# A recurrent decoder layer on Trainium2: a new order of the side work in a group of sixteen steps

## The chip, the cores and the metric

The kernel runs on one core of a Trainium2 chip. The metric is the device time in microseconds of one execution; the median of several executions counts. The engines are TensorE (PE; its weight loads are PEld), VectorE (DVE), ScalarE (ACT), GpSimd (POOL) and SyncE (SP), which issues most of the DMAs.

## What is computed

A decoder layer over x of 16 batches x 128 time steps x 256 features. Its first part is a recurrence over the 128 time steps, beside it attention and a mixture of experts:

```python
def step(carry, inp):
    h_ssm = silu(h_ssm @ A.T + bxt)                  # state of 64
    y_ssm = h_ssm @ Cw.T + Cb + dxt
    r = sigmoid(i_r + h_r); z = sigmoid(i_z + h_z)   # h_* = h_rnn @ W_hh.T, GRU state of 128
    n = tanh(i_n + r * h_n)
    h_rnn = (1 - z) * n + z * h_rnn
    fused = g0 * y_ssm + g1 * (h_rnn @ proj_w.T)     # g = sigmoid(x @ gate_w.T)
```

Then x1 = layernorm(x + fused); a retention layer (queries of x1, keys and values of ctx_1024, a rotary embedding, a decay mask) gives x2 = layernorm(x1 + ret); eight experts with the top 2 of 8 and a capacity of 320 rows work on x2; the sum is normalised once more.

## The kernel before, in words

The work is ordered by hand. A group g has CH = 16 time steps: two tiles j = 0, 1 of ST = 8 steps x 16 batches = 128 rows. There are 8 groups. Each engine runs its own list: in a group, for every step s, first the step of the recurrence (`rec`), then the side work that the list has for s. Groups 0 and 1 stand alone, because keys and values are computed in them; groups 2 to 7 are a loop (A and M true). Engines meet only by semaphores, which count up.

One step of the recurrence: TensorE multiplies the state (`at_w`) and the two halves h1, h2 of the GRU state (float16, high and low) by the weights (rec, L783 to L812); ScalarE takes two sigmoids (L549, L550) and the tanh (L552); VectorE does a scan (L1131), two small ops (L1133, L1134), the state product (L1137), the scans that give h1 and hist (L1142, L1143), and h2 (L1145). TensorE's part of step s needs VectorE's h2 of step s - 1. So side work stands in front of the next step on the same engine.

Side work of group g in the loop, by the step behind which it stands:

- TensorE (`iteration`, L917): `fin_a` and `fin_b` of tile 2g - 1 at 0 and 1 and of tile 2g at 12 and 13 (output of both states, and at the end of `fin_b` the gate matmuls into the bank TB); `scores` of chunk g - 2 at 2, 4; inputs of the next tiles at 3, 5, 14, 15; `x1_tr` at 6; `mix` at 7, 9; `q_proj` at 8, 10, both halves into TB; `back` at 11. `fin_b` at 13 waits for the rotation (qmul_ready).
- VectorE (L1280): stats and norm of x1 at 0, 1 and 4, 5; `fuse` at 2, 3 and 14, 15; `decay` at 5; two `residual` at 10; two pairs of rotation products at 11, 12; statistics and variance of x2 at 13; `logits` and `norm_2` at 14, 15, one tile each.
- ScalarE (L612): `gates` at 1, 13; `ret_high` at 6; x1T copies at 7; x1R copy at 11; `q_high` at 14.
- GpSimd (L431), in one queue and as soon as its inputs are there: `rstd_1` twice, `ret_low`, `rot_q` (two sums of 128x256), `rstd_2`, `q_low` (two differences).

Names used below: TB, FB, QB, SC are PSUM banks; `pv_ready`, `res_ready`, `x1_ready` and the like are the semaphores that a named result raises. The kernel splits float32 operands in float16 high and low halves: `q_high`, `q_low`, `ret_high`, `ret_low`. The order around it:

```python
            with act.Fori(2, CHUNKS) as g:
                iteration(g, True, True)
            gates(TILES - 1)
            ret_high(CHUNKS - 2)
            x1T_copy(CHUNKS - 1)
```

Of the kernel before, what the change touches and what calls it, by code (L numbers as in the profile page):

```python
# [14 lines left out]
SSM, RNN = 64, 128  # L15
# [26 lines left out]
V_SLOTS = (2, 4, 6, 7, 9, 11)  # L42
# [4 lines left out]
LO_STEP = (2, 3, 4, 5, 6, 6, 7, 7, 8, 8, 9, 9, 10, 13, 13, 14)  # L47
# [14 lines left out]
def mk_decoder_kernel(nc, xtok, xT, ctxT, consts, AbE, BwT, CwE, DwT, W_ihT, b_rows, bsel, iota, W_hhT, projT,  # L62
# [5 lines left out]
    with ExitStack() as ctx:  # L68
# [93 lines left out]
        rs1 = sb("rs1", [P, 1])  # L162
        x1 = [sb(f"x1_{j}", [P, D]) for j in range(2)]
# [68 lines left out]
        def quarter(a1, a2, p):  # L232
# [164 lines left out]
        def _(pool):  # L397
# [16 lines left out]
            def rot_q(c):  # L414
                for h, op in enumerate((ALU.subtract, ALU.add)):
                    pool.wait_ge(q["qmul_ready"], 2 * c + h + 1)
                    pool.tensor_tensor(qr[:, h, :], tm[:, 2 * h, :], tm[:, 2 * h + 1, :], op).then_inc(q["qr_ready"], 1)  # L417

            def q_low(c):
                for h in range(HD):  # L420
                    pool.wait_ge(q["qh_ready"], 2 * c + h + 1)
                    pool.tensor_tensor(qp[1][:, h, :], qr[:, h, :], qp[0][:, h, :], ALU.subtract).then_inc(q["ql_ready"], 1)
# [8 lines left out]
            def iteration(g, A, M):  # L431

                if A:
                    rstd_1(2 * g - 2)
                    if not M:
                        rot_k(3)
                    rstd_1(2 * g - 1)
                if A and not M:

                    for i in range(8):  # L440
                        pool.dma_start(ybuf[i * 4 * P:(i + 1) * 4 * P, :].rearrange("(k p) d -> p k d", p=P),
                                       zero[:].unsqueeze(1).to_broadcast([P, 4, D])).then_inc(q["zrow"], 16)
                if M:
                    ret_low(g - 2)
                if A:
                    rot_q(g - 1)
                if M:
                    rstd_2(g - 2)
                if A:
                    q_low(g - 1)  # L450
# [8 lines left out]
            iteration(0, False, False)  # L459
# [3 lines left out]
            iteration(1, True, False)  # L463
            with pool.Fori(2, CHUNKS) as g:
                iteration(g, True, True)
            rstd_1(TILES - 2)
            rstd_1(TILES - 1)
            ret_low(CHUNKS - 2)
            rot_q(CHUNKS - 1)
# [75 lines left out]
        def _(act):  # L545
# [8 lines left out]
            def gates(n):  # L554

                act.wait_ge(q["fin_ready"], n + 1)
                for i in range(2):
                    nc.scalar.activation(gxs[:, i:i + 1], TB[:, i:i + 1], ACT.Sigmoid, bias=gb[:, i:i + 1]).then_inc(q["gx_ready"], 1)

            def x1T_copy(c):  # L560
                act.wait_ge(q["x1tr_ready"], c + 1)
                for h in range(HD):
                    nc.scalar.copy(x1T[:, h, :], TB[:, h * 256:(h + 1) * 256]).then_inc(q["x1T_ready"], 1)
# [1141 lines left out]
```

## Time and profile before

| | |
|---|---|
| median of 3 executions | 502.61 us (502.03 to 504.88) |
| profiled execution, its own time | 504.28 us |
| its span, first to last instruction | 502.4 us |
| mean granted TensorE clock | 0.896 of full speed |
| busy: PE, PEld, DVE, ACT, POOL | 404.9, 309.5, 382.6, 235.6, 138.5 us |
| first sigmoid of the recurrence, last one | 11.1 us, 279.3 us |

The three parts of the span are the recurrence with its side work (to 281 us), attention's rest and the routing (to about 330 us), and the experts and the final norm. A row of a timeline says when an instruction began, how long it took, and in brackets how long its engine had been idle before and what released it. Rows of one kind that follow each other are merged (x2, x48).

### The profile page before, as it was taken

How to read it: one execution, taken by the hardware profiler on the slowest of the kernel's cores; microseconds unless marked ns; L12 is line 12 of the kernel's file. 1: busy time of each engine (PE TensorE's matmuls, PEld its weight loads, DVE VectorE, ACT ScalarE, POOL GpSimd, SP SyncE). 2: the span in 40 equal slices, each digit the busy share in tenths (PEclk: the TensorE clock that was granted, in tenths of full speed). 3: DMA queues.
4: the chain of work that ended last, by engine and by line, in shares of the span. 5: the costliest groups of instructions: out<-in, count | busy, mean ns of one | idle time of the engine just before them, and what ended most of it. 6: DMA issues, size and time to landing. Idle time of an engine off the chain costs nothing.

```text
span 502.4 us, 13430 instructions
## 1 busy us (share of the span) xinstructions
PE 404.9 (81%) x4675; PEld 309.5 (62%) x4675; DVE 382.6 (76%) x1575; ACT 235.6 (47%) x803; POOL 138.5 (28%) x207
## 2 busy tenths in 40 slices
PE   7978899899999999999899766128999999998000
PEld 4535676687877878778687655115677777776000
DVE  5578888988879788797987555875789888894184
ACT  1454166433333332333333133334998888972053
POOL 0023332211113121121211221153124554413284
PEclk8889989999999999999999586557999999999555
DMA  8940128110111102011020000016534565101482
GB/s 289 359 172 1 33 74 294 31 37 1 52 32 31 52 0 80 3 31 52 0 76 1 23 3 22 22 35 213 168 137 149 182 214 198 47 7 48 145 281 104
DMA packets 38238, 46.49 MB, mean 93 GB/s; under 512 B 4283, under 2 KB 32702, under 8 KB 38202
## 3 DMA queue, kind: packets, MB, share of 16 engines
q1 hardware_dynamic: 34474, 35.93, 21.5%
q0 software_dynamic: 3200, 9.40, 5.9%
q10 hardware_dynamic: 528, 0.69, 0.5%
q8 instruction: 21, 0.34, 0.3%
q14 instruction: 15, 0.12, 0.1%
HBM read 35.04 MB, written 11.01 MB: 92 GB/s over the span
## 4 chain that ended last, share of the span: by engine, by line
PE 43%; DVE 27%; ACT 11%; issue 10%; POOL 3%; DMA 3%; ACTq 0%; SPq 0%; DVEq 0%; POOLq 0%
PE bank L758 42%; DVE h L1142 3%; DVE ub L1131 3%; DVE mb L1133 3%; ACT arena L676 2%; ACT arena L667 2%; DVE h L1145 2%; DVE hist L1143 2%; DVE st L1205 1%; ACT arena L705 1%; ACT kp L676 1%; DVE vp L1480 1%; DVE tm L1174 1%; DVE mb L1134 1%; PE bank L1056 1%
## 5 line engine op out<-in xcount | busy, mean ns | idle before, releaser
L549 ACT ACTIVATE rzb<-bank 128x32 f32<-128x32 f32 x128 | 25.4, 198 | 104.0 <-PE bank L758 102.7
L758 PE MATMUL bank<-h,whp 128*128 128x32 f16 x1143 | 62.0, 184 | 5.1 <-DVE h L1142 2.6
L758 PE MATMUL bank<-arena 128*128 128x320 f16 x384 | 57.0, 307 | 1.4 <-DVE arena L1527 1.4
L1131 DVE TENSOR_TENSOR_SCAN ub<-rzb,bank 128x32 f32<-128x32 f32 x128 | 28.0, 219 | 39.5 <-ACT rzb L549 38.4
L758 PE MATMUL bank<-arena,kp 128*128 128x320 f16 x384 | 54.5, 299 | 0.0
L758 PEld LDWEIGHTS bank<-h,whp 128*128 128x128 f16 x1143 | 41.7, 96 | 15.4 <-DVE h L1145 3.5
L552 ACT ACTIVATE nb<-ub 128x16 f32<-128x16 f32 x128 | 27.9, 218 | 47.4 <-DVE ub L1131 47.4
L758 PEld LDWEIGHTS bank<-arena 128*128 128x128 f16 x384 | 38.2, 101 | 16.9 <-DVE arena L1527 1.6
L758 PEld LDWEIGHTS bank<-hsb,at_w 66*64 66x64 f32 x256 | 25.2, 137 | 34.7 <-DVE hsb L1137 23.2
L758 PEld LDWEIGHTS bank<-arena,kp 128*128 128x128 f16 x384 | 37.3, 98 | 14.1
L758 PE MATMUL bank<-hsb,at_w 66*64 66x16 f32 x256 | 36.9, 220 | 6.9 <-DVE hsb L1137 6.7
L1133 DVE TENSOR_SCALAR mb<-rzb,hneg,hup 128x16 f32<-128x16 f32 x128 | 41.1, 321 | 0.0
L503 POOL DMA_INDIRECT ybuf<-arena,six x24 | 24.2, 1009 | 58.0 <-DVE arena L1542 53.1
L705 ACT ACTIVATE arena<-bank,b1s 128x320 f32<-128x320 f32 x64 | 32.2, 540 | 16.5 <-PE bank L758 16.4
L1531 DVE CAST arena<-arena 128x320 f16<-128x320 f32 x64 | 20.9, 326 | 19.8 <-ACT arena L705 18.1
L417 POOL TENSOR_TENSOR qr<-tm 128x256 f32<-128x256 f32 x16 | 11.6, 725 | 84.8 <-DVE tm L1174 84.8
L407 POOL TENSOR_TENSOR ve<-mv,epst 128x1 f32<-128x1 f32 (+1 forms) x24 | 5.0, 208 | 103.4 <-DVE mv L1162 78.9
L667 ACT ACTIVATE arena<-wbuf 128x1024 bf16<-128x1024 f32 x32 | 33.4, 1058 | 0.0
L1142 DVE TENSOR_TENSOR_SCAN h<-nb,mb 128x32 f16<-128x32 f32 x128 | 31.6, 247 | 1.5
L1535 DVE TENSOR_TENSOR arena<-arena 128x320 f16<-128x320 f32 x64 | 30.4, 485 | 0.0
L758 PE MATMUL bank<-xin_t,wih 128*128 128x128 f32 x192 | 28.6, 286 | 1.4 <-DMA bw<-in_BwT 1.4
L1145 DVE TENSOR_TENSOR h<-hist,h 128x16 f16<-128x16 f32 x128 | 25.4, 198 | 4.5
(209 smaller groups left out, 935.5 us busy)
## 6 DMA issues: line engine op xcount, KB each, us to landing
wbuf<-in_w SPq DMA_DIRECT2D x16, 1024.0 KB, 5.9
ybuf<-zero POOLq DMA_DIRECT2D x8, 512.0 KB, 7.2
wbuf<-ybuf SPq DMA_DIRECT2D x16, 256.0 KB, 5.5
xin_t<-in_xT SPq DMA_DIRECT2D x16, 128.0 KB, 2.2
arena<-in_ctxT SPq DMA_DIRECT2D x4, 512.0 KB, 7.0
xfin_t<-in_xT SPq DMA_DIRECT2D x16, 128.0 KB, 2.2
xres<-in_xtok SPq DMA_DIRECT2D x16, 128.0 KB, 2.1
x_d<-x SPq DMA_DIRECT2D x8, 256.0 KB, 2.3
```

The lines of the kernel that those rows point to most:

```text
L503: pool.indirect_dma_start(ybuf[:, :], bass.IndirectOffsetOnAxis(ap=six[0:m, col], axis=0), yt[e % 2][0:m, c, :], None, bounds_check=2 * S ...
L549: nc.scalar.activation(od(rzb[:]), RZ[j][:, s * 2 * B:(s + 1) * 2 * B], ACT.Sigmoid).then_inc(q["r_ready"], 1)
L552: nc.scalar.activation(od(nb[:]), od(ub[:]), ACT.Tanh).then_inc(q["n_ready"], 1)
L667: nc.scalar.activation(wjunk[p % 2].rearrange("p (a b) -> p a b", a=src.shape[1]), src, ACT.Square, accum_out=wsum2[j][:, p // 2, p % 2:p ...
L705: nc.scalar.activation(h32[:, f % 4, :], bank[2 + f % 4][:, 0:CAP], ACT.Relu, bias=b1s[j][:, f:f + 1]).then_inc(q["h32_ready"], 1)
L758: return nc.tensor.matmul(out_, lhsT, rhs, start=start, stop=stop, skip_group_check=True)
L1131: nc.vector.tensor_tensor_scan(ub[:], rzb[:, 0:2 * B], NS[j][:, s * 32:s * 32 + 32], 0.0, ALU.mult, ALU.add).then_inc(q["npre_ready"], 1)
L1133: nc.vector.tensor_scalar(ev(mb[:]), od(rzb[:, 2 * B:4 * B]), hneg[:, 0:1], hup[:, 0:1], ALU.mult, ALU.add)
L1142: nc.vector.tensor_tensor_scan(h1[:], nb[:], mb[:], 0.0, ALU.mult, ALU.add).then_inc(q["h1_done"], 1)
L1145: nc.vector.tensor_tensor(h2[:], h_of(j, s), od(h1[:]), ALU.subtract).then_inc(q["h2_done"], 1)
L1531: nc.vector.tensor_copy(hp[0][:, f, :], h32[:, f % 4, :]).then_inc(q["h_hi"], 1)
L1535: nc.vector.tensor_tensor(hp[1][:, f, :], h32[:, f % 4, :], hp[0][:, f, :], ALU.subtract).then_inc(q["h_lo"], 1)
```

## The change

It replaces the list of the loop by a new one on four engines, and changes a few helpers. In steps of the new loop:

- TensorE: `fin_a` 0 and 11, `fin_b` 1 and 13, `scores` 2, 3, inputs 4, 6, 14, 15, `x1_tr` 5, `mix` 7, 10, `q_proj` 8, 9, `back` 12.
- Gate matmuls move from the end of `fin_b` to `fin_a`, into columns 384, 385 of RZ[j]; the bias matmul goes the other way. `in_a` waits for the gates.
- `q_proj` writes its second half to FB; each half raises q_ready. `fin_a` of tile 2g waits for all rotation products.
- VectorE: products one by one at 8, 9, 9, 10; `residual` 10, 11; stats of x2 12, variance 13; `fuse` 1, 2 and 13, 14; stats of x1 0, 3; `norm_1` of the second tile 4; `ret_low` 6 (it was GpSimd's); both `logits` 15.
- ScalarE: `norm_1` of the first tile at 2, `norm_2` of both tiles at 15, as Identity with scale and bias; x1T copies at 6 and 7; x1R copy 12; `q_high` 13, 14. GpSimd computes the biases (`shift_1`, `shift_2`).
- GpSimd: `rot_q` and `q_low` wait for h2 of steps 11, 12, 13, 14 (`behind`). The two `rot_q` wait for all products.
- In group 1 the value matmuls of step 9 go to 10, three low halves go to step 11, the tables to 8, projections and products to 8, 9 and 9, 10.

```diff
-V_SLOTS = (2, 4, 6, 7, 9, 11)
+V_SLOTS = (2, 4, 6, 7, 10, 11)
-LO_STEP = (2, 3, 4, 5, 6, 6, 7, 7, 8, 8, 9, 9, 10, 13, 13, 14)
+LO_STEP = (2, 3, 4, 5, 6, 6, 7, 7, 8, 8, 11, 11, 11, 13, 13, 14)
...
-            def ret_low(c):
-                pool.wait_ge(q["rh_ready"], c + 1)
-                pool.tensor_tensor(rp[1][:], ret[:], rp[0][:], ALU.subtract).then_inc(q["rl_ready"], 1)
+            def rot_q(c, h):
+                pool.wait_ge(q["qmul_ready"], 2 * c + 2)
+                op = (ALU.subtract, ALU.add)[h]
+                pool.tensor_tensor(qr[:, h, :], tm[:, 2 * h, :], tm[:, 2 * h + 1, :], op).then_inc(q["qr_ready"], 1)
...
+            def shift_2(c):
+                pool.tensor_tensor(ng2[:], zero[:, 0:2], mv2[:, :, 0], ALU.subtract).then_inc(q["neg2"], 1)
+                pool.wait_ge(q["neg2"], c + 1)
+                pool.wait_ge(q["rstd2"], c + 1)
+                pool.tensor_tensor(nm2[:], ng2[:], rs2[:], ALU.mult).then_inc(q["shift2"], 1)
+            def behind(g, s):
+                pool.wait_ge(q["h2_done"], CH * g + s + 2)
+            def iteration(g):
+                rstd_1(2 * g - 2)
+                shift_1(g)
+                rstd_1(2 * g - 1)
+                behind(g, 11)
+                rot_q(g - 1, 0)
+                behind(g, 12)
+                rot_q(g - 1, 1)
+                behind(g, 13)
+                q_low(g - 1, 0)
+                rstd_2(g - 2)
+                shift_2(g - 2)
+                behind(g, 14)
+                q_low(g - 1, 1)
...
+            def norm_1(g):
+                act.wait_ge(q["shift1"], g - 1)
+                nc.scalar.activation(x1[0][:], s1b[:], ACT.Identity, bias=nm1[:], scale=rs1[:]).then_inc(q["x1_ready"], 1)
+            def norm_2(c, j):
+                if j == 0:
+                    act.wait_ge(q["shift2"], c + 1)
+                    act.wait_ge(q["lg_ready"], 2 * c + 2)
+                nc.scalar.activation(x2[:, bass.ds(2 * c + j, 1), :].rearrange("p o (h d) -> p (o h) d", h=HD), halves((QB, SC)[j]), ACT.Identity,
+                                     bias=nm2[:, j:j + 1], scale=rs2[:, j:j + 1]).then_inc(q["x2_ready"], 1)
...
             def in_a(n, j):
+                if not isinstance(n, int) or n >= 2:
+                    pe.wait_ge(q["gx_ready"], 2 * n - 2)
...
                 mm(FB[:, 0:D], xfin_t[j][:, 0, :], dw[:, 0, :], False, False)
+                for h in range(HD):
+                    last = mm(RZ[j][:, 3 * P:3 * P + 2], xfin_t[j][:, h, :], gw[:, h, :], h == 0, h == 1)
+                last.then_inc(q["gate_ready"], 1)
+            def fin_b(n, j):
+                mm(FB[:, 0:D], xfin_t[j][:, 1, :], dw[:, 1, :], False, True)
                 mm(FB[:, D:2 * D], ones16[:], bzq[:, RNN:RNN + D], False, False)
...
-                last.then_inc(q["fin_ready"], 1)
+                mm(FB[:, D:2 * D], od(hist[j][:]), pw[:], False, True).then_inc(q["fin_ready"], 1)
...
-                    last = mm(TB[:, o * 256:(o + 1) * 256], wq[:, h, o * P:(o + 1) * P], x1T[:, h, :], h == 0, h == 1)
-                if o == 1:
-                    last.then_inc(q["q_ready"], 1)
+                    last = mm((TB, FB)[o][:, 0:256], wq[:, h, o * P:(o + 1) * P], x1T[:, h, :], h == 0, h == 1)
+                last.then_inc(q["q_ready"], 1)
...
                 if part == 0:
                     dve.wait_ge(q["gx_ready"], 2 * n + 2)
+                    dve.wait_ge(q["fin_ready"], n + 1)
...
                     dve.wait_ge(q["fuse_a"], n + 1)
+                    if not isinstance(n, int):
+                        dve.wait_ge(q["x1_ready"], n)
...
             stats_1(n)
             norm_1(n, 1)
+            ret_low(c - 1)
```

## Rows read from the trace of the kernel before

**Rows 1.** the profile's page, part 4: the chain that ended last, by engine
```profile
PE 43%; DVE 27%; ACT 11%; issue 10%; POOL 3%; DMA 3%; ACTq 0%; SPq 0%; DVEq 0%; POOLq 0%
```

**Rows 2.** timeline, group 3, L549: start us, us taken, what [idle before <-releaser]
```profile
128.51 0.20 ACT L549 ACTIVATE rzb<-bank 128x32 f32<-128x32 f32 x1 [0.96 <-PE bank L758]
...
132.41 0.20 ACT L549 ACTIVATE rzb<-bank 128x32 f32<-128x32 f32 x1
...
139.41 0.20 ACT L549 ACTIVATE rzb<-bank 128x32 f32<-128x32 f32 x1 [0.96 <-PE bank L758]
...
141.56 0.20 ACT L549 ACTIVATE rzb<-bank 128x32 f32<-128x32 f32 x1 [1.09 <-PE bank L758]
...
148.55 0.20 ACT L549 ACTIVATE rzb<-bank 128x32 f32<-128x32 f32 x1 [0.96 <-PE bank L758]
...
150.84 0.20 ACT L549 ACTIVATE rzb<-bank 128x32 f32<-128x32 f32 x1 [0.89 <-PE bank L758]
...
152.57 0.20 ACT L549 ACTIVATE rzb<-bank 128x32 f32<-128x32 f32 x1 [0.96 <-PE bank L758]
...
155.02 0.20 ACT L549 ACTIVATE rzb<-bank 128x32 f32<-128x32 f32 x1
...
159.11 0.20 ACT L549 ACTIVATE rzb<-bank 128x32 f32<-128x32 f32 x1 [0.96 <-PE bank L758]
```

**Rows 3.** timeline, step 12 of the group, VectorE's h2
```profile
152.09 0.17 DVE L1145 TENSOR_TENSOR h<-hist,h 128x16 f16<-128x16 f32 x1
```

**Rows 4.** timeline, step 6: GpSimd's ret_low and VectorE's h2
```profile
140.55 0.67 POOL L426 TENSOR_TENSOR rp<-ret,rp 128x256 f16<-128x256 f32 x1 [1.68 <-ACT rp L578]
140.66 0.59 DVE L1145 TENSOR_TENSOR h<-hist,h 128x16 f16<-128x16 f32 x1
```

**Rows 5.** timeline of TensorE, step 11: back and the next state matmul
```profile
149.08 1.19 PE L758 MATMUL bank<-rgi,sT 128*128 128x136 f32 x8 [0.53 <-DVE sT L1198]
150.21 0.29 PE L758 MATMUL bank<-hsb,at_w 66*64 66x16 f32 x2
```

**Rows 6.** timeline, steps 12 and 13: L1133 and GpSimd's rot_q
```profile
151.28 0.33 DVE L1133 TENSOR_SCALAR mb<-rzb,hneg,hup 128x16 f32<-128x16 f32 x1
...
153.01 0.72 POOL L417 TENSOR_TENSOR qr<-tm 128x256 f32<-128x256 f32 x1 [1.44 <-DVE tm L1174]
153.01 0.76 DVE L1133 TENSOR_SCALAR mb<-rzb,hneg,hup 128x16 f32<-128x16 f32 x1
```

**Rows 7.** timeline, step 13: gate matmuls, next state matmul, the gates
```profile
153.95 0.50 PE L758 MATMUL bank<-gw,xfin_t 128*128 128x2 f32 x4
...
154.38 0.29 PE L758 MATMUL bank<-hsb,at_w 66*64 66x16 f32 x2
...
154.49 0.41 ACT L558 ACTIVATE gxs<-bank,gb 128x1 f32<-128x1 f32 x2 [1.15 <-PE bank L758]
```

**Rows 8.** timeline of VectorE, steps 13 and 15: statistics and a norm of x2
```profile
154.34 0.88 DVE L1205 BATCH_NORM_STATS2 st<-bank 128x6 f32<-128x128 f32 x4
...
159.26 0.54 DVE L1224 TENSOR_SCALAR x<-bank,mv,rs 128x256 f32 x1
```

**Rows 9.** line L1185 (VectorE's ret_low, after the loop): ns min/median/max
```profile
L1185 DVE TENSOR_TENSOR rp<-ret,rp x1: 426/426/426, 304.5 to 304.5; 128x256 f16<-128x256 f32 x1
```

**Rows 10.** timeline of TensorE, step 7: mix and the next state matmul
```profile
141.40 1.36 PE L758 MATMUL bank<-rp,vp 128*128 128x32 f16 x48
142.69 0.29 PE L758 MATMUL bank<-hsb,at_w 66*64 66x16 f32 x2
```

**Rows 11.** timeline of ScalarE near the end: two norms of the output
```profile
483.19 1.09 ACT L750 ACTIVATE arena<-arena,nm,rs 128x256 f32<-128x256 f32 x2 [1.12 <-POOL nm L535]
```

**Rows 12.** line L1278, group 1: low halves of the values (keys: 743 median, x8)
```profile
L1278 DVE SCALAR_TENSOR_TENSOR vp<-arena,scl,vp x8: 741/746/826, 78.5 to 95.6; 128x512 f16<-128x512 f32 x8
```

**Rows 13.** timeline of VectorE behind the loop: norm of x1
```profile
290.84 0.75 DVE L1167 TENSOR_SCALAR x<-s1b,mv,rs 128x256 f32<-128x256 f32 x1 [0.93 <-POOL rs L409]
```

**Rows 14.** groups by line and form, ScalarE: xcount | busy us, mean ns
```profile
L651 ACT ACT_TABLE_LOAD x1 | 1.3, 1283 | 2.3 <-issue 2.3
```

More of the change, by code:

```diff
@@ L428, in rstd_2, with shift_1 @@
             def rstd_2(c):
                 rstd(q["var2"], q["eps2"], rs2[:], None, q["rstd2"], (ve2[:], mv2[:, :, 1]), c + 1)
[L431 to L450, printed above, removed]
+            def shift_1(g):
+                pool.tensor_tensor(ng1[:], zero[:, 0:1], mv1[:, 0:1], ALU.subtract).then_inc(q["neg1"], 1)
+                pool.wait_ge(q["neg1"], g - 1)
+                pool.wait_ge(q["rstd1"], 2 * g - 1)
+                pool.tensor_tensor(nm1[:], ng1[:], rs1[:], ALU.mult).then_inc(q["shift1"], 1)
@@ L452, in _, with second @@
+            def second():
+                rstd_1(0)
+                rot_k(3)
+                rstd_1(1)
+                for i in range(8):
+                    pool.dma_start(ybuf[i * 4 * P:(i + 1) * 4 * P, :].rearrange("(k p) d -> p k d", p=P),
+                                   zero[:].unsqueeze(1).to_broadcast([P, 4, D])).then_inc(q["zrow"], 16)
+                for h in range(HD):
+                    rot_q(0, h)
+                for h in range(HD):
+                    q_low(0, h)
             pool.memset(ones[:], 1.0).then_inc(q["init_p"], 1)
@@ L458, in _ @@
                 rot_k(i)
-            iteration(0, False, False)
             pool.wait_ge(q["nrm_done"], 1)
             pool.tensor_tensor(inv[:], nrm[:], mhalf[:], ALU.pow).then_inc(q["inv_done"], 1)
-            iteration(1, True, False)
+            second()
             with pool.Fori(2, CHUNKS) as g:
-                iteration(g, True, True)
+                iteration(g)
             rstd_1(TILES - 2)
             rstd_1(TILES - 1)
-            ret_low(CHUNKS - 2)
-            rot_q(CHUNKS - 1)
+            for h in range(HD):
+                rot_q(CHUNKS - 1, h)
             rstd_2(CHUNKS - 2)
@@ L683, in _ @@
             exponentials(0, 0, TILES - 4)
-            q_high(CHUNKS - 1)
+            q_high(CHUNKS - 1, 0)
+            q_high(CHUNKS - 1, 1)
             x1R_copy(CHUNKS - 1)
@@ L915, in sums, with iteration, early @@
                 last.then_inc(q["nsum"], 1)
-            def iteration(g, A, M, has_next):
+            def iteration(g, has_next):
+                for s in range(CH):
+                    rec(g, s // ST, s % ST)
+                    if s == 0:
+                        fin_a(2 * g - 1, 1)
+                    if s == 1:
+                        fin_b(2 * g - 1, 1)
+                    if s in (2, 3):
+                        scores(g - 2, s - 2)
+                    if s == 4:
+                        in_a(2 * g + 1, 1)
+                    if s == 5:
+                        x1_tr(g - 1)
+                    if s == 6:
+                        in_b(1)
+                    if s in (7, 10):
+                        mix(g - 2, (s - 7) // 3)
+                    if s in (8, 9):
+                        q_proj(g - 1, s - 8)
+                    if s == 11:
+                        pe.wait_ge(q["qmul_ready"], 2 * g)
+                        fin_a(2 * g, 0)
+                    if s == 12:
+                        back(g - 2)
+                    if s == 13:
+                        fin_b(2 * g, 0)
+                    if has_next and s == 14:
+                        in_a(2 * g + 2, 0)
+                    if has_next and s == 15:
+                        in_b(0)
+            def early(g, A):
                 for s in range(CH):
```

224 lines of the change are left out of this document (126 added, 98 removed).

## The prediction

> **What bounds the kernel now.** I read the page first. Its chain of work gives TensorE 43% and VectorE 27%, with neither engine full [rows 1]. This is a chain of waits: 128 dependent steps of a recurrence. So I took the start of ScalarE's first sigmoid (L549) as the clock of a step and read group g = 3 of the loop (six looped groups, 2 to 7, repeat it within 0.1 us). The group takes 159.11 - 128.51 = 30.60 us for 16 steps [rows 2]. The step from 150.84 to 152.57 takes 1.73 us, and 141.56 to 148.55 is four steps at 1.75 [rows 2]. So 1.73 us is the floor: sigmoid at 0, VectorE's first scan at 0.30, h2 starting at 1.25 [rows 3], h2's matmuls, next sigmoid. Sixteen floors are 27.7 us. The group loses 2.9 us in named places, and 6 groups hold 17 us: this is all the change can win in the loop.
>
> The losses, as interval after a step minus 1.73:
> - Step 6, 2.15 (+0.42): GpSimd's ret_low starts at 140.55 for 0.67 us, and h2, due at 140.66, takes 0.59 instead of 0.17 [rows 4].
> - Step 11, 2.29 (+0.56): TensorE waits 0.53 us for the residual before `back` [rows 5]; the next step's state matmul is behind it.
> - Step 13, 2.45 (+0.72): GpSimd's rot_q begins together with L1133, which takes 0.76 us instead of 0.27; then `fin_b`, which waited for the rotation, still has the gate matmuls in it when the state is ready [rows 6, 7].
> - Steps 14 and 15, together 4.09 (+0.63) [rows 2], then step 0 (2.03, +0.30) and step 1 (1.87, +0.14), together 3.90 [rows 2]: VectorE does statistics (0.88 us) and in each of two steps fuse, logits and a 0.54 us norm [rows 8]. Room for VectorE's extras in a step is about 0.7 us, from h2's end to the next scan; above it the step grows one for one.
>
> **The change, part by part, per looped group.**
> *Step 6/7.* ret_low goes from GpSimd to VectorE: h2 is free, -0.42. But `mix` in step 7 needs it at once. VectorE starts it 0.09 after h2's start, at 1.33, it takes 0.43 [rows 9], and a matmul follows 0.06 behind: `mix` starts at 1.82, 0.09 after the next sigmoid. Today it starts 0.16 before the sigmoid, and at 1.29 us from its start to the state matmul's it just fits [rows 10]. So step 7 grows by 0.24. Net -0.18.
> *Steps 8 to 10.* Query halves go to two banks, so a rotation product starts behind each half; one, two, one products (0.33 us pitch) plus a residual stay within about 0.05 of the room. TensorE's two projections (1.1 us) fit. Net 0; cover: VectorE's 0.7 us. Without it, each extra 0.1 us is paid.
> *Steps 11, 12.* `fin_a` takes the gate matmuls (0.43 us pitch [rows 7]) and gives up the bias one (0.21): about 1.37 us on TensorE, 0.08 more than `mix`, so step 11 costs 1.84. `back` goes behind step 12, where the last residual is ready about as the sigmoid starts; its 1.13 us [rows 5] end 0.02 late. Step 12 costs 1.78 against 1.73. Net -0.41.
> *Step 13.* The rotation is over three steps earlier, `fin_b` loses the gates, gates come from `fin_a` of step 11 (0.41 us [rows 7] on ScalarE behind q_high's 0.4; room there is 1.1). Four statistics in step 12 make the scan of 13 late by 0.06. GpSimd's rot_q now waits for h2: start 1.25 + 0.17 + 0.08 = 1.50, 0.72 long, over at 0.49 of the next step. In step 12 of today one runs from the sigmoid at 150.84 on and is over at 0.72; L1133 took 0.33, and the step was still 1.73 [rows 2, 6]. So it costs nothing with 0.2 in hand. Step 13: 1.80, net -0.65. VectorE's fuse is split over 13 and 14, and 14 drops to 1.75, -0.20.
> *Step 15.* Here is the new cost. The norms of x2 go to ScalarE, after step 15's tanh and before the next group's first sigmoid, and they wait for both logits (same PSUM banks). VectorE issues logits behind h2 with dynamic addresses: about 1.44 and 1.62, 0.22 long like today's, over at 1.84. ScalarE then sees the semaphore (0.06), computes an address (0.1) and runs two Identity activations of 128x256. Today two such take 1.09 us [rows 11], the next op about 0.09 earlier; from PSUM they may be 0.1 to 0.2 cheaper (the 128x256 copies out of PSUM are 0.37). I take 0.95: next sigmoid at 2.95, and 0.05 for q_low(1), which GpSimd can only start behind the rstd_2 and shift_2 chain, so near 0.03 of step 15, over at 0.70. Step 15: 3.0 instead of 2.14, **+0.86**. Bounds: 2.2 if the wait costs VectorE's old excess only, 3.3 if nothing overlaps.
> *Steps 0, 1.* VectorE no longer has a norm in step 15: step 0 is 1.74 (-0.29); TensorE is ahead of the late sigmoid, so `fin_a` is covered. Step 1 has a shorter `fin_b`: 1.77 (-0.10). x1's norm on ScalarE in step 2 (0.59) is ready as VectorE wants s1b at 1.33; the shift chain on GpSimd is over some 0.6 us before it. Rests of 0.01 to 0.03 in steps 2 to 5 and 9: +0.07.
> Sum without step 15: -0.18 - 0.41 - 0.65 - 0.20 - 0.29 - 0.10 + 0.07 = -1.76; six groups, -10.6. Step 15 counts in five (behind the last the norms cover matmuls): +4.3. **Loop: -6.3.**
> *Second group (g = 1).* Low halves of keys and values (0.74 us each, 16 of them [rows 12]) move from steps 9, 10 to 11, so three stand together there, and tables join two of them in step 8: 2.2 and 2.05 us against 0.7 of room. The value matmuls go to neighbouring steps 10 and 11, where they overlap VectorE's excess less. Followed step by step, +1.4 at step 11, +0.75 at the end after the faster step 13. Bounds 0 and +2.
> *After the loop.* `fin_a` of the last tile no longer waits for a fuse: -0.9; x1's norm, 0.75 today beside ret_low on GpSimd instead of 0.41 [rows 13], -0.34; GpSimd's first rotation sum waits for all four products: +0.62. **-0.6**, bounds -1.3 and +0.6. First group: its changes end in a wait for GpSimd's rot_k, 0. SP's and POOL's queues: loads of xfin wait for fuses that come earlier; the store of x2 waits for ScalarE's norms, needed only a group later.
> Sum: -6.3 + 0.75 - 0.6 = **-6.1 us**. The profiled execution took 504.28, of which 502.40 is span; it becomes 498.2. The median, 1.7 lower at 502.61, becomes **496.5**.
>
> One cost the rows leave open: var_2 (step 13) reads SBUF as q_low begins. Held like h2 it pushes fuse, +0.5 a group, to 499.5. The Trainium skill (GPSIMD Engine Reference, Specifications) names as contended only VectorE instructions in a 2-port mode or with two SBUF inputs; the row of L1133 (0.76) agrees; by that, this cost would be 0.
>
> **Rivals.**
> - *ScalarE's hold is cheap.* Step 15 near 2.2: 0.8 x 5 = 4 less, 492.5. For: activations run beside TensorE's lead. Against: the sigmoid stands behind both norms in one queue. 15%.
> - *It balances out.* Two collisions a group left (0.44 each, 5.3 in all), or the second group at +2 with var_2 held: 500.5 to 502. 17%.
> - *GpSimd still meets VectorE (slower).* Place: the four big subtractions of steps 11 to 15, started behind h2. If the wait and its arithmetic let each begin late enough to sit on L1133 or h2, each costs about 0.44 [rows 4, 6]: 1.76 x 6 = 10.6, less 0.3 that the sum has for it, 506.8. It decides from about 0.5 us of lateness; my slack is 0.2, and nil for q_low(1). For: q_low(1) waits for a long chain. Against: these waits are short today (0.08). 10%.
> - *Identity needs its own table (slower).* A table load takes 1.28 us [rows 14]; the trace has two in all, this one ahead of the sigmoids and one at the exponentials. Two swaps and back per group are 5.1 us, 31 in all, 527. Square and copies ran beside the sigmoid without one, Identity never did. 3%. The Trainium skill (ScalarE: Activation LUTs, Table sets) says that the cheap functions, identity among them, are in every set; by that this rival falls.
> - *It does not do what it says* is in the second one: the parts move costs, and only the sum moves time.
>
> **Numbers.** Forecast case 55%, 494 to 499.5. With cheap hold 15%: faster by over 0.5% (about what a measurement of this kernel can tell from no change; below 500.1) 0.70. Same 0.17, slower 0.13. The range 491 to 502.5 leaves out the two slower cases and a little at the bottom.
>
> **What would show it.** In the changed profile: step 6 at 1.73 with h2 at 0.17; a TensorE wait for ret_low and 2.0 in step 7; 1.84 in step 11, 1.8 in step 13; L1133 never above 0.35 in the loop; after step 15 some 3.0, ScalarE waiting for logits, two norms of 0.5; group length near 29.7; group 1 longer. Wrong: step 15 below 2.5, L1133 or h2 above 0.5 us, or a table load in the loop.

## The result, and the profile after

The changed kernel takes 512.82 us in the median of 4 executions (509.92 to 517.02). The kernel before takes 503.75 us in 4 executions beside it. The ratio is 1.018, with a 95% interval of 1.0133 to 1.0228: the change costs 1.8%, where 1.2% less time was forecast. The profiled execution took 509.92 us, with a span of 508.1 us; it is the fastest of the four. Here and below a median is of all executions, while a ratio leaves out those over 1.5% above the fastest of their kernel (two each of kernels 1 and 4, four of kernel 5), so that it can lie up to 0.4% beside the quotient of the medians.

The page's list of the chain that ended last, by engine, looks almost like the old one [rows 1]:

```profile
PE 44%; DVE 23%; ACT 13%; issue 12%; POOL 3%; DMA 3%; ACTq 1%; SPq 0%; DVEq 0%; POOLq 0%
```

VectorE lost 4 points, as the change meant it to; ScalarE and "issue" took 2 each, TensorE 1, and none of them stands out. So I measured steps again, from one first sigmoid (L571 now) to the next. The loop's groups, which were equal within 0.13 us before, no longer are:

| group | 0 | 1 | 2 | 3 | 4 | 5 | 6 | 7 (15 steps) |
|---|---|---|---|---|---|---|---|---|
| before, us | 45.19 | 41.47 | 30.7 | 30.6 | 30.6 | 30.6 | 30.6 | 28.44 |
| after, us | 43.29 | 43.48 | 33.58 | 31.26 | 30.26 | 33.83 | 31.25 | 27.08 |

The stretches of the loop show what differs. The columns are start and end, the busy time (with the number of instructions) of PE, PEld, DVE, ACT and POOL, the granted TensorE clock, the DMA share and GB/s. The kernel before, from group 2 on:

```profile
98.00:129.00 31.00, 29.18 (x455) 24.36 (x456) 25.86 (x139) 10.47 (x60) 5.81 (x11) 1.00 0.09 27
129.00:159.00 30.00, 28.59 (x454) 23.82 (x453) 25.26 (x138) 10.15 (x56) 5.76 (x11) 1.00 0.11 35
159.00:190.00 31.00, 29.11 (x458) 24.17 (x455) 26.26 (x142) 10.67 (x60) 5.77 (x11) 1.00 0.11 34
190.00:220.00 30.00, 28.59 (x451) 23.86 (x451) 25.27 (x138) 10.15 (x56) 5.77 (x11) 1.00 0.12 35
220.00:251.00 31.00, 29.23 (x459) 24.23 (x457) 26.26 (x141) 10.54 (x60) 5.77 (x11) 1.00 0.11 34
```

The same view of the changed kernel, one row for each of groups 2 to 6:

```profile
98.00:131.00 33.00, 32.26 (x460) 26.33 (x461) 24.75 (x138) 10.84 (x60) 5.84 (x14) 0.90 0.12 34
131.00:163.00 32.00, 30.74 (x460) 25.24 (x459) 24.41 (x137) 12.32 (x63) 5.80 (x14) 0.95 0.12 37
163.00:193.00 30.00, 28.93 (x453) 23.93 (x453) 24.43 (x137) 11.32 (x62) 5.80 (x14) 1.00 0.11 33
193.00:227.00 34.00, 32.94 (x457) 27.02 (x457) 24.71 (x137) 11.75 (x62) 5.85 (x14) 0.85 0.11 32
227.00:258.00 31.00, 29.95 (x456) 24.57 (x455) 24.41 (x137) 11.33 (x62) 5.80 (x14) 0.94 0.10 32
```

Before, the granted clock is 1.00 in every row. After, it is 1.00 only in group 4, which is also the only short one. The order of the clocks (1.00, 0.95 and 0.94, 0.90, 0.85) is the order of the lengths (30.26, 31.26 and 31.25, 33.58, 33.83).

**Where the clock falls.** The timeline of TensorE at the start of group 5, over the first two steps:

```profile
193.03 0.50 PE L815 MATMUL bank<-gw,xfin_t 128*128 128x2 f32 x4
194.18 0.29 PE L815 MATMUL bank<-hsb,at_w 66*64 66x16 f32 x2 [0.66 <-DVE hsb L1215]
194.42 0.61 PE L815 MATMUL bank<-h,whp 128*128 128x32 f16 x9
194.85 1.20 PE L815 MATMUL bank<-dw,xfin_t 128*128 128x256 f32 x2
...
196.05 1.06 PE L815 MATMUL bank<-pw,hist 128*128 128x256 f32 x2
```

and the windows around it, with the columns as above:

```profile
190.00:194.00 4.00, 3.53 (x37) 2.95 (x36) 2.33 (x15) 1.81 (x8) 1.03 (x4) 1.00 0.35 98
194.00:198.00 4.00, 3.82 (x39) 2.63 (x40) 2.74 (x15) 0.96 (x8) 1.08 (x4) 0.57 0.00 0
```

TensorE has run ahead: `fin_a` (192.08 to 193.53) began 1.2 us before the late sigmoid (193.27) and is over long before step 0 has given TensorE its next input, the state product `hsb` at 194.13. So it stands still for 0.66 us. In the kernel before this matmul follows `fin_a` without a stop. Behind that the two 128x256 matmuls of `fin_b` take 1.20 us; at 192.59, ahead of the stop, the same form takes 0.60. This is the lower of the two levels, 1.2 instead of 2.4 GHz. `fin_b` is on the path then, and step 1 takes 2.84 us instead of 1.76. The timeline of ScalarE shows why the sigmoid was late, and the long step 1 (195.02 to 197.86):

```profile
192.36 1.02 ACT L605 ACTIVATE x<-bank,nm,rs 128x256 f32 x2 [1.21 <-DVE lg L1306]
193.27 0.20 ACT L571 ACTIVATE rzb<-bank 128x32 f32<-128x32 f32 x1
...
195.02 0.20 ACT L571 ACTIVATE rzb<-bank 128x32 f32<-128x32 f32 x1 [0.98 <-PE bank L815]
...
197.86 0.20 ACT L571 ACTIVATE rzb<-bank 128x32 f32<-128x32 f32 x1 [1.76 <-PE bank L815]
```

The first row is the hold, which the prediction had priced at +0.86 for step 15: two Identity norms behind `logits`, 1.02 us long, with the sigmoid of step 0 behind them.

A second place is step 11. Group 4 (first three rows) has the clock at 1.00, group 5 (the others) loses it:

```profile
182.34 0.42 DVE L1255 TENSOR_TENSOR tm<-bank,cq 128x256 f32<-128x256 f32 x1
183.01 0.67 PE L815 MATMUL bank<-cwe,hsb 66*128 66x256 f32 x2 [0.26 <-DVE tm L1255]
183.52 0.60 PE L815 MATMUL bank<-dw,xfin_t 128*128 128x256 f32 x2
...
214.27 0.67 PE L815 MATMUL bank<-cwe,hsb 66*128 66x256 f32 x2 [0.26 <-DVE tm L1255]
214.77 0.97 PE L815 MATMUL bank<-dw,xfin_t 128*128 128x256 f32 x2
...
216.96 2.16 PE L815 MATMUL bank<-rgi,sT 128*128 128x136 f32 x8
```

`fin_a` waits for the last rotation product of step 10. The product ends at 182.76, as the h matmuls do, and `fin_a` starts 0.25 behind it: step 11 takes 2.26. In group 5 `back` takes 2.16 us instead of 1.17, and steps 11, 12 and 13 take 3.12, 2.73 and 2.59 instead of 2.26, 1.74 and 1.82.

**The 5.7 us of span, term by term.** Group 2 without the fall of the clock is 31.38 us (step 0 as 2.24, from the first experiment below), and groups 3 to 6 are 30.26 each, as group 4 is: 152.4 for five, against 153.0 before. The clock has added 160.18 - 152.4 = 7.8 us to them, and 4.01 - 2.74 = 1.3 to step 10 of group 1. The rest of group 1 is +0.7, group 7 is -1.4, and behind the last sigmoid it is 222.7 instead of 223.1, -0.4. Group 0 and what is ahead of it are 1.6 shorter, which is scatter: group 0 took 43.3 in one profile and 46.2 in another of one and the same kernel (the hold alone, below). Sum: -0.6 + 7.8 + 1.3 + 0.7 - 1.4 - 0.4 - 1.6 = +5.8.

This explains one execution, the fastest. The medians differ by 9.1 us, and the other three executions have a mean granted clock of 0.864 to 0.877 where the profiled one has 0.883. More clock lost in them would fit; there is no profile of them.

### The profile page after: what moved, and what is told of

It is laid out like the page before. It is cut to its first block, busy times and chain, and to the rows that moved or that the text cites. A ratio compares the mean times of both kernels' runs of the same rounds, so it can differ in the third digit from the quotient of the medians.

```text
span 508.1 us, 13545 instructions
## 1 busy us (share of the span) xinstructions
PE 414.0 (81%) x4675; PEld 315.0 (62%) x4675; DVE 373.3 (73%) x1564; ACT 242.8 (48%) x821; POOL 139.2 (27%) x224
## 4 chain that ended last, share of the span: by engine, by line
PE 44%; DVE 23%; ACT 13%; issue 12%; POOL 3%; DMA 3%; ACTq 1%; SPq 0%; DVEq 0%; POOLq 0%
PE bank L815 43%; DVE h L1220 2%; DVE ub L1209 2%; ACT arena L723 2%; DVE mb L1211 2%; ACT arena L732 2%; ACT kp L732 2%; ACT arena L762 2%; ACT rzb L571 1%; DVE hist L1221 1%; DVE tm L1255 1%; DVE vp L1587 1%; DMA wbuf<-ybuf 1%; DMA bw<-in_BwT 1%; DVE mb L1212 1%
## 5 line engine op out<-in xcount | busy, mean ns | idle before, releaser
L571 ACT ACTIVATE rzb<-bank 128x32 f32<-128x32 f32 x128 | 25.5, 199 | 111.3 <-PE bank L815 111.2
L815 PE MATMUL bank<-h,whp 128*128 128x32 f16 x1143 | 63.2, 185 | 4.2 <-DVE h L1220 2.6
L1211 DVE TENSOR_SCALAR mb<-rzb,hneg,hup 128x16 f32<-128x16 f32 x128 | 36.7, 286 | 0.0
L517 POOL DMA_INDIRECT arena<-x_d,gix x24 | 26.6, 1108 | 7.4 <-issue 6.3
```

Source lines behind the costliest of these rows:

```text
L517: pool.indirect_dma_start(xe[e % 2][0:m, c, :], None, x2_d[:, :], bass.IndirectOffsetOnAxis(ap=gix[0:m, col], axis=0), bounds_check=S - 1, ...
L571: nc.scalar.activation(od(rzb[:]), RZ[j][:, s * 2 * B:(s + 1) * 2 * B], ACT.Sigmoid).then_inc(q["r_ready"], 1)
L815: return nc.tensor.matmul(out_, lhsT, rhs, start=start, stop=stop, skip_group_check=True)
L1211: nc.vector.tensor_scalar(ev(mb[:]), od(rzb[:, 2 * B:4 * B]), hneg[:, 0:1], hup[:, 0:1], ALU.mult, ALU.add)
```

## The experiments

The theory is that the moves themselves gain a little, and that the loss is TensorE's clock, which falls behind the stops that the change makes: ScalarE's hold at the border of two groups, and `fin_a`'s wait at step 11. The rivals are that the hold and the wait cost by their own length, and that GpSimd still meets VectorE. No experiment changes what is computed; 2, 3 and 9 add matmuls or copies that nothing reads. "Before" is the kernel before, on the same chip; experiments 1 to 4 share one chip, 5 to 9 another. The change itself was not measured again on either, so its +1.8% stands beside these ratios and not in a row with them.

**1. The hold goes.** ScalarE writes the norms of x2 behind step 0 of the next group. For that, group 2 is taken out of ScalarE's loop, and the norms of the last looped group stand behind it. A part of the edit:

```diff
+                    if late and s == 0:
+                        norm_2(g - 3, 0)
+                        norm_2(g - 3, 1)
...
-                    if s == 15:
-                        norm_2(g - 2, 0)
-                        norm_2(g - 2, 1)
```

> The changed kernel, with ScalarE's two norms of x2 behind the first step of the next group instead of behind the last step of this one, so that no sigmoid stands behind the wait for the logits. Theory A (the hold of 1.1 us at the group's border leaves TensorE idle, and the granted clock then falls to 1.2 GHz for a stretch): the interval after step 15 goes from 2.9 to 1.8 us and the stretches at half clock in groups 2 to 7 are gone; the looped groups take 29.2 us each, the time falls by about 14 us, to 498. Theory B (the half-clock stretches have nothing to do with the hold): only 1.1 x 5 = 5.5 us are gained, 507, and half-clock stretches remain in the loop.

Measured: 505.25 us (10 executions) against 505.43, ratio 0.9989 [0.9935, 1.0043]. Step 15 is 1.74, step 1 is 1.73 or 1.74 in every looped group, and none loses the clock at its start. Step 0 grew to 1.98: `fin_a` with the gate matmuls is 1.37 us long, and no late sigmoid hides it now. Undisturbed groups are 29.32. Two groups still lose the clock, both at step 11 (3.14 and 3.17 instead of 2.26). So neither expectation came true: no fall is left at the borders, but falls are left in the loop, and the time is 505 instead of 498. The windows of this kernel, groups 4 and 5:

```profile
161.00:193.00 32.00, 31.59 (x461) 26.37 (x460) 24.73 (x138) 11.70 (x61) 5.89 (x14) 0.89 0.11 33
193.00:222.00 29.00, 28.59 (x453) 23.77 (x450) 24.13 (x136) 11.70 (x61) 5.83 (x14) 1.00 0.12 36
```

**2. The hold stays, the stop goes.** TensorE gets four unused 512-column matmuls where it would stand still.

```diff
                     if s == 0:
                         fin_a(2 * g - 1, 1)
+                        for i in range(4):
+                            mm(TB[:], ones16[:], no)
```

> The changed kernel with four matmuls of 512 columns into a free bank behind fin_a of step 0 (0.9 us of work that nobody reads, where TensorE is idle during ScalarE's hold). Theory A: the hold stays at 2.9 us, but the half-clock stretches at the starts of groups are gone; looped groups are 30.3 us each (up to 0.2 more for the extra matmuls), the time falls by 5 to 9 us, to 504 to 508. Theory B: half-clock stretches remain, the time is 512 to 514.

Measured: 503.41 us (10) against 505.43, ratio 0.9994 [0.9946, 1.0042]. The hold is as long as ever (step 15: 2.88 to 2.90, in group 2 3.09), and step 1 is 1.73 to 1.77 in every looped group. One group loses the clock, at step 11 (32.85), the others of groups 3 to 6 take 30.25. With more work on TensorE and a hold as long as ever the kernel stands level with the one before: the hold's length alone doesn't make these moves slower than the old order.

**3. The hold in the kernel before.** ScalarE waits for h2 behind step 15 and makes four unused copies.

```diff
+                    if M and s == 15:
+                        act.wait_ge(q["h2_done"], CH * g + CH + 1)
+                        for i in range(4):
+                            nc.scalar.copy(junk[:, i, :], zero[:])
```

> The kernel before with a hold of ScalarE alone: behind step 15 of each looped group it waits for h2 and makes four copies of 128x256 that nobody reads, 1.3 us. Theory A: the interval after step 15 grows by about 1.0 us to 3.1, and beside that half-clock stretches appear behind it in some groups, 1 us or more each: slower by 7 to 14 us against before. Theory B: 1.0 x 5 = 5 us slower, the granted clock stays at 1.00 in the loop.

Measured: 512.92 us (6) against 505.43, ratio 1.0146 [1.0065, 1.0226]. Step 15 is 3.09 to 3.22 instead of 2.14, and in three groups step 1 is 3.06 to 3.29 instead of 1.87, with the clock down. Those groups take 33.31, 33.56 and 33.56, an undisturbed one 31.24. The hold alone, with nothing else of the change, brings a loss. By this profile 3.2 us of it are the hold's own length (undisturbed groups are 0.65 longer, group 2 is 0.9 longer, group 7 0.3 shorter) and 6.7 us the three falls; it is the slowest of the six executions, so most of them lost less to the clock.

**4. GpSimd doesn't wait for h2.** `behind` does nothing.

```diff
             def behind(g, s):
-                pool.wait_ge(q["h2_done"], CH * g + s + 2)
+                pass
```

> The changed kernel without GpSimd's waits for h2 (its sums and differences begin as soon as their inputs are there). If these waits do what their name says, L1133's op or h2 is held in one to three places a group again, 0.3 to 0.5 us each: slower by 2 to 9 us than the changed kernel. If GpSimd was never the cost in the new order, the time stays within 1 us of the changed kernel's 512.

Measured: 509.54 us (10) against 505.43, ratio 1.0053 [1.0001, 1.0106]. Undisturbed groups are 30.70 instead of 30.26: step 12 is 1.86 instead of 1.74, step 13 is 2.15 instead of 1.82. The timeline of this kernel, GpSimd's rows each with the VectorE row beside it:

```profile
187.22 1.42 POOL L421 TENSOR_TENSOR qr<-tm 128x256 f32<-128x256 f32 x2 [11.51 <-DVE tm L1255]
187.58 0.40 DVE L1211 TENSOR_SCALAR mb<-rzb,hneg,hup 128x16 f32<-128x16 f32 x1
...
192.40 0.67 POOL L425 TENSOR_TENSOR qp<-qr,qp 128x256 f16<-128x256 f32 x1 [3.76 <-ACT qp L594]
192.51 0.59 DVE L1223 TENSOR_TENSOR h<-hist,h 128x16 f16<-128x16 f32 x1
```

With the waits, in the changed kernel, GpSimd starts behind h2 and is over in time, and L1211 keeps its 0.27:

```profile
186.27 0.18 DVE L1223 TENSOR_TENSOR h<-hist,h 128x16 f16<-128x16 f32 x1
186.53 0.73 POOL L421 TENSOR_TENSOR qr<-tm 128x256 f32<-128x256 f32 x1 [1.45 <-DVE h L1223]
...
187.28 0.27 DVE L1211 TENSOR_SCALAR mb<-rzb,hneg,hup 128x16 f32<-128x16 f32 x1
```

So the waits are worth 0.44 us a group. The rival that GpSimd still meets VectorE falls. The forecast of the time failed: 2 to 9 us more than the change were expected, and it is 3.3 less (509.54 against 512.82, on another chip, with ranges that overlap). The missing waits can't be the reason. The clock can: within the loop this profile lost it in group 2 alone, and the mean over the ten executions is 0.893. This kernel has kept both stops (0.64 to 0.85 us at the start of groups 3 to 7, 0.25 at step 11), so how often the clock falls behind them varies by more than a single repair gives back.

**5. The products come earlier.** Two pairs, at steps 8 and 9, so that `fin_a` at 11 waits for none of them.

```diff
-                    if s == 8:
-                        turn(g - 1, 0, 0)
-                    if s == 9:
-                        turn(g - 1, 0, 1)
-                        turn(g - 1, 1, 0)
+                    if s in (8, 9):
+                        rotate(g - 1, s - 8)
                     if s == 10:
-                        turn(g - 1, 1, 1)
                         residual(g - 2, 0)
```

> The changed kernel with the rotation products in pairs behind steps 8 and 9 instead of one, two, one behind 8, 9 and 10, so that fin_a of step 11 finds them done. Theory A (any stop of TensorE, also the 0.3 us in front of fin_a of step 11, can be followed by a stretch at 1.2 GHz): step 11 goes from 2.26 to 1.84 us, no half-clock stretch begins at a step 11 any more, those at the groups' starts remain; undisturbed groups 29.85 us; 3 to 6 us faster than the changed kernel. Rival: the stop at step 11 is only its own 0.42 x 6 = 2.5 us, and half-clock stretches still begin there.

Measured: 507.59 us (12) against 506.08, ratio 1.0003 [0.9957, 1.0049]. Step 11 is 1.94, step 9 is 1.84 (it was 1.73), the undisturbed group 30.01. No group loses the clock at step 11; groups 2, 3, 4 and 6 lose it at their start. So 1.94 is what `fin_a`'s length alone costs, and its wait cost 0.32.

**6. Both stops go** (1 and 5 together; no new edit).

> e1 and e5 together: ScalarE's norms behind step 0 of the next group, products at 8 and 9. Theory A: both stops are gone, no half-clock stretch in groups 2 to 7, each 28.9 us; about 10 us faster than before. Rival (the clock falls because the shorter list leaves TensorE less busy on the whole): half-clock stretches somewhere in groups 2 to 7, time 498 to 503.

Measured: 498.5 us (6) against 506.08, ratio 0.9831 [0.9781, 0.9881]: now 1.7% faster than before. Groups 3 to 6 take 29.10 each. Kernel 5, on the same chip, takes 9.1 us more; 4.9 of them are the hold's own length (0.91 in groups 3 to 6, 1.4 in group 2, less 0.1 in group 7), the rest goes with the mean clock, 0.889 there and 0.899 here. That the shorter list as a whole leaves TensorE too little to do falls with it: groups 3 to 7 keep the full clock. Windows, from group 1 on:

```profile
81.00:99.00 18.00, 15.08 (x122) 11.41 (x120) 14.89 (x63) 8.85 (x35) 2.71 (x4) 0.91 0.33 111
99.00:131.00 32.00, 31.32 (x453) 25.72 (x454) 24.53 (x137) 10.63 (x59) 5.83 (x14) 0.89 0.09 27
131.00:161.00 30.00, 29.77 (x468) 24.80 (x467) 25.29 (x143) 11.70 (x61) 5.78 (x14) 1.00 0.13 39
161.00:190.00 29.00, 28.77 (x455) 24.11 (x454) 24.32 (x138) 11.69 (x61) 5.82 (x14) 1.00 0.12 36
```

What is left of lower clock up to the last sigmoid lies ahead of step 0, in groups 0 and 1 and at the start of group 2, where neither edit reaches; kernels 1, 7 and 8 had none at the start of group 2 in their profiles, with the same code there. Against the kernel before, each on its own chip, the change stands at +1.8%, kernel 4 with the same two stops at +0.5%, the kernels with one stop gone at -0.1 and 0.0, with both gone at -1.7%.

**7. Two more repairs.** The norms of x2 one behind step 0 and one behind step 1; projections at 7 and 9, `mix` at 8 and 10, so that `ret_low` has a step of its own; both x1T copies at 6. A part of the edit:

```diff
-                    if s in (7, 10):
-                        mix(g - 2, (s - 7) // 3)
-                    if s in (8, 9):
-                        q_proj(g - 1, s - 8)
+                    if s in (8, 10):
+                        mix(g - 2, (s - 8) // 2)
+                    if s in (7, 9):
+                        q_proj(g - 1, (s - 7) // 2)
```

> e6 with the two norms split over steps 0 and 1, and with mix and projections exchanged (projections 7 and 9, mix 8 and 10, both x1T copies behind step 6), so that mix no longer waits for ret_low. Expected: step 0 from 1.98 to 1.75, step 7 from 2.02 to 1.75, groups of 28.4 us, 3 us faster than e6. If the waits only move (projection waits for the copies, scores for the norm), groups of 28.7 to 28.9 us.

Measured: 496.1 us (6) against 506.08, ratio 0.9804 [0.976, 0.9849]. Step 7 is 1.73 instead of 2.02, groups 4 to 6 are 28.81 to 28.83. The 2.4 us to kernel 6 are within what the two sets of six executions scatter. Step 0 stays 1.98, so it was not the length of the two norms but `fin_a`: its matmuls run from 183.95 on, and the state matmul stands behind them at 185.32.

**8. Group 1 as well.** Its three low halves spread over steps 9, 10 and 11, the tables at 9, the products at 10 and 11. A part of the edit:

```diff
-LO_STEP = (2, 3, 4, 5, 6, 6, 7, 7, 8, 8, 11, 11, 11, 13, 13, 14)
+LO_STEP = (2, 3, 4, 5, 6, 6, 7, 7, 8, 8, 9, 10, 11, 13, 13, 14)
```

> e8 with the low halves of group 1 spread over steps 9, 10, 11 one each, the tables at 9 and the products at 10 and 11. If the three low halves together at step 11 and the tables with two of them at step 8 cost what the prediction said (0.75 us) and the stop of TensorE there calls a half-clock stretch, group 1 goes from 42.8 to 41.5 us and the time falls by 1 to 2 us. Rival: the same work costs the same wherever it stands, 0.

Measured: 496.26 us (6) against 506.08, ratio 0.9792 [0.9747, 0.9838]. Step 9 of group 1 is 2.19 instead of 3.02, but steps 11 and 12 take back 0.3; the group is 42.17 instead of 42.68. From kernel 7 the time can't be told apart; 1 to 2 us less were expected, and 41.5 for the group.

**9. The hold with the stop filled, in the kernel before**, and the hold alone once more beside it. This is kernel 3 with the four unused matmuls of kernel 2.

```diff
                     if A and s == 0:
                         fin_a(2 * g - 1, 1)
+                        if M:
+                            for i in range(4):
+                                mm(TB[:], ones16[:], no)
```

> The kernel before with the same hold of ScalarE behind step 15, and now also with four unused 512-column matmuls on TensorE behind fin_a of step 0 of the looped groups, where TensorE stood still. Clock theory: the hold itself stays (step 15 at 3.1), but no stretch at half clock follows it, step 1 is 1.87 in every looped group, the looped groups are 31.25 to 31.65 long, and the time is 5 to 8 us below that of the kernel with the hold alone, about 508. If the lower clock came from the hold's length or from anything else than TensorE's standing still: two or three groups of 33.3 as before, and no gain over the kernel with the hold alone.

> The kernel before with the hold alone, once more, so that the filled one stands beside it on one chip. Both theories: step 15 at 3.1; a median near 513, 1.5% above the kernel before. Clock theory: step 1 at 3.1 with a stretch at half clock in two to four of the looped groups, not always the same ones.

Measured, against 504.6: filled 510.22 us (6), ratio 1.0125 [1.0085, 1.0166]; hold alone 513.1 (6), ratio 1.0181 [1.0145, 1.0218]. Windows of the hold alone, a group without and a group with a fall:

```profile
98.00:128.00 30.00, 28.22 (x451) 23.73 (x451) 24.68 (x132) 11.25 (x60) 5.82 (x11) 1.00 0.09 25
128.00:161.00 33.00, 30.95 (x453) 25.54 (x452) 25.75 (x139) 11.10 (x62) 5.79 (x11) 0.90 0.10 32
```

and of the filled one, the same two groups:

```profile
98.00:131.00 33.00, 31.23 (x475) 25.72 (x476) 26.87 (x146) 10.88 (x62) 5.83 (x11) 1.00 0.09 26
131.00:163.00 32.00, 30.10 (x462) 24.71 (x463) 26.54 (x142) 12.23 (x65) 5.78 (x11) 1.00 0.11 33
```

In the filled kernel groups 2 to 6 have 1.00 and step 1 is 1.85 in every looped group, while step 15 is still 3.09 to 3.23. The hold alone had added a stop of 0.40 us behind `fin_a` at the start of groups 3 to 7, and the fill takes this one away and no other. The timeline of its TensorE shows the fill in the place of the stop, and the matmul of `fin_b` at its short time behind it:

```profile
163.92 1.02 PE L763 MATMUL bank<-zero,ones 96*128 96x512 f16 x4
164.87 0.29 PE L763 MATMUL bank<-hsb,at_w 66*64 66x16 f32 x2
...
165.34 0.68 PE L763 MATMUL bank<-dw,xfin_t 128*128 128x256 f32 x2
```

The gain of 2.9 us is less than the 5 to 8 expected. The fill costs 0.2 in step 0 (1.93 instead of 1.72) in five groups and 0.9 in group 2, 1.9 in all; and the profile of the hold alone lost the clock in two groups, 2.3 us each. The executions scatter by about as much as the gain (2.6 us between the means, plus or minus 2.6), but the mean clock doesn't: it is 0.894 to 0.912 in the six with the fill and 0.871 to 0.895 in the six without. Of the loss that is left (1.25%), the profile shows 4.9 us as the loop's own length with the hold and the fill.

**All executions together.** The profile is one execution, but each execution has its mean granted clock:

| kernel | executions | mean granted clock | median, us |
|---|---|---|---|
| before (chip of 1 to 4) | 25 | 0.901 | 505.43 |
| the change | 4 | 0.874 | 512.82 |
| hold gone (1) | 10 | 0.885 | 505.25 |
| stop filled (2) | 10 | 0.899 | 503.41 |
| products earlier (5) | 12 | 0.889 | 507.59 |
| no waits of GpSimd (4), both stops kept | 10 | 0.893 | 509.54 |
| both stops gone (6) | 6 | 0.899 | 498.5 |
| before with hold (3) | 6 | 0.888 | 512.92 |
| the same once more (9) | 6 | 0.885 | 513.1 |
| before with hold, filled (9) | 6 | 0.903 | 510.22 |

The change has the lowest clock of all, but it was measured by itself; kernel 4 with the same stops has more than kernels 1 and 5 with one of them gone. So what a single repair gives back of the clock isn't shown by this table. On one chip two pairs show it: the hold with and without the fill (0.903 and 0.885), and kernels 6 and 5 (0.899 and 0.889), of which 6 has no hold.

## Why the prediction was wrong, point by point

The reading of single steps held, step 11 apart. Forecast and measured intervals of a looped group at full clock (group 4):

| step | before | forecast | measured |
|---|---|---|---|
| 0 | 2.03 | 1.74 | 1.73 |
| 1 | 1.87 | 1.77 | 1.76 |
| 6 | 2.15 | 1.73 | 1.74 |
| 7 | 1.76 | 2.00 | 2.02 |
| 11 | 2.29 | 1.84 | 2.26 |
| 12 | 1.74 | 1.78 | 1.74 |
| 13 | 2.45 | 1.80 | 1.82 |
| 14 | 1.96 | 1.75 | 1.79 |
| 15 | 2.14 | 3.00 | 2.90 |

**The step that failed is "the new cost" of step 15, and with it the sum, which had no term for TensorE's clock.** I priced ScalarE's hold by its own length, +0.86 (measured +0.76), and took the rest of the queue as free: "TensorE is ahead of the late sigmoid, so `fin_a` is covered". It is covered, but being ahead means that TensorE then has nothing to do, and that has a price which the sum had not. The clock costs 7.8 us in groups 2 to 6 of the profile, which is more than the whole forecast gain: 3.0 in the first steps of groups 3, 5 and 6, right behind the hold, 2.6 at step 11 of group 5, and 2.2 in the first steps of group 2. These last stand behind stops of 0.25 and 0.23 us that the kernel before has there too, with no fall in its profile; what brought this fall is not shown. That the stop behind the hold brings falls is shown by experiments 2 and 9, which fill it, by 3, which makes it in the other kernel, and by 1 and 6, which take it away and have no fall at the borders of groups 3 to 7. Not every such stop brings one: experiment 4 keeps the hold, and its profile shows no fall behind it. My question to each covered operation was what hides it; I didn't ask what the hidden engine does until it is wanted.

**The second failed step is step 11.** "Steps 8 to 10, net 0" looked at VectorE's room alone. It was right for those steps (1.73, 1.73, 1.76). But the last product ends at 182.76, just as the sigmoid of step 11 starts, TensorE is free at the same moment, and it starts 0.25 later. This is not what one wait costs: in step 0 of group 5 VectorE's `hsb` is over at 194.13, and the matmul that waits for it alone starts at 194.18. In front of `fin_a` of step 11 three waits stand in a row (qmul_ready, the load of xfin, fuse_b), and by the trace it passes the first at 182.84 and the second at 182.96, both behind the product. The 1.84 for step 11 came from `fin_a`'s length, with no wait for that product at all: the length makes 1.94 of it, and the wait 0.32 more. The wait is a stop too, and the clock fell there in group 5 (2.6 us of the 7.8).

**Smaller terms.** "Rests" in steps 2 to 5 and 9 were +0.07; steps 2 to 5 measure 0.28 more than before, with 1.87 in step 2 and 1.85 in step 4 as the largest; which of the moved operations does it was not tried. Group 2 is 1.1 longer than the later ones (2.24 in step 0, 3.10 in step 15), which I had taken as equal. At full clock the loop is 2.0 us shorter than before, where 6.3 were forecast; of the 4.3 between, step 11 makes 2.3, steps 2 to 5 1.2 and group 2 1.1, step 15 takes back 0.5, and 0.2 lie in small terms. Group 1 at full clock is +0.7 against +0.75 forecast; the fall at its step 10 adds 1.3 (kernels 1, 2 and 7 have the same wait and no fall there). TensorE waits ahead of it, in step 9, for VectorE, which has the tables and two low halves in one step. The timeline of TensorE, with the value matmuls at the lower clock in the last row:

```profile
81.88 0.39 PE L815 MATMUL bank<-hsb,at_w 66*64 66x16 f32 x2 [1.42 <-DVE hsb L1215]
82.21 0.53 PE L815 MATMUL bank<-h,whp 128*128 128x32 f16 x9
82.55 3.26 PE L815 MATMUL bank<-wv,arena 128*128 128x256 f32 x8
```

Behind the loop it is -0.4 against -0.6. At full clock, by these terms, the span would be 508.1 - 7.8 - 1.3 = 499.0, and 1.6 of that is the scatter ahead of group 1: 500.6, a gain of 1.8 of 502.4 instead of 6.1. So without the clock the number of the second rival, that it balances out, would have come out (500.5 to 502, for the median). That would have been luck: its mechanism, two collisions a group or a second group at +2, is not what these terms show.

**The other rivals.** ScalarE's hold is not cheap (2.90, not 2.2). GpSimd meets VectorE nowhere in the loop: L1211 is 0.27 to 0.33 and h2 0.17 or 0.18 where [rows 4, 6] had 0.59 and 0.76. The cost that the prediction left open, the variance of x2 beside `q_low`, did not come (step 14: 1.79 against 1.75 forecast, not 0.5 more). But it wasn't put to the test, since the one is over as the other begins, and what they do to each other stays open (the changed kernel, step 13 of group 4):

```profile
188.18 0.28 DVE L1299 BATCH_NORM_AGGREGATE mv<-st 128x2 f32<-128x12 f32 x2
188.43 0.67 POOL L425 TENSOR_TENSOR qp<-qr,qp 128x256 f16<-128x256 f32 x1 [1.18 <-DVE h L1223]
```

Identity needs no table of its own. The groups by line and form of ScalarE have two loads, as before, one of them at L706, ahead of the first sigmoid, where [rows 14] had it, and the other behind the loop:

```profile
L706 ACT ACT_TABLE_LOAD x1 | 1.3, 1283 | 2.3 <-issue 2.3
```

The side on which I had the time was wrong, and the slower rival that I did price (GpSimd, 506.8) was another mechanism than the one that decided.

## What to carry to other kernels

When a change makes one engine late at a point where TensorE has run ahead, price two things: the lateness, and what TensorE costs afterwards if it stands still meanwhile. Look for it in the granted clock of each stretch before and after, not in the mean of the whole execution (0.896 and 0.883 here, which looks like little). One profile doesn't tell how often the clock falls; the mean clock of several executions of both kernels on one chip tells more. A late hold should go where another engine's work is long enough to cover it, and where that can't be had, matmuls that nobody reads can cost less than the stop. Where a result is ready just as an engine comes free, count the waits that stand in a row in front of its next instruction: 0.25 us for three of them here, 0.05 where one stands alone.

## What was not expected of the hardware

- The granted clock fell to its lower level behind stops of TensorE of 0.26 and 0.66 us; from 190 to 194 us, with a part of the second stop in it, it was busy for 3.53 of 4.00 us, and the clock was still 1.00 there. The Trainium skill (TensorE: Matmul & The Clock Gate, "A second HAM failure mode: psum-queue depth-cycling") tells of a kernel in which short idle times between groups of matmuls made the clock swing between its two levels; the rows here agree in kind.
- It doesn't fall each time. Stops of the same length, in groups with the same instructions, are followed by the lower clock in some groups and not in others, and which ones differs between executions (groups 3, 4 and 6 in one profile of the hold alone, groups 3 and 5 in the other). The kernel before even stands still for longer in a looped group, 0.53 us at step 11 [rows 5] and three times more, 1.39 us in all where the changed kernel has 0.91 in group 5, and its profile shows no fall from group 2 to step 13 of group 7:

```profile
152.99 0.70 PE L758 MATMUL bank<-dw,xfin_t 128*128 128x256 f32 x2 [0.41 <-DVE tm L1174]
158.29 0.29 PE L758 MATMUL bank<-hsb,at_w 66*64 66x16 f32 x2 [0.21 <-DVE hsb L1137]
159.35 0.67 PE L758 MATMUL bank<-cwe,hsb 66*128 66x256 f32 x2 [0.24 <-DVE s1b L1155]
```

So neither the longest stop nor the sum of them decides, and what tells these cases apart is left open.

- The kernel before scatters from 501.2 to 509.1 us on one chip. A part of it may lie in the first group: the profiles of all kernels here have step 0 of group 0 at 2.4 in some and at 3.9 to 4.4 in others.
